# Banded attention: the output projection as plain fp32 matmuls, and four step tables laid out anew

## The chip, the core and the metric

The kernel is one program on one core of a Trainium2 chip. The metric is the device time of one execution in microseconds (us), as the median of the runs shown. Engines are named as in the profile: PE (TensorE matmul), PEld (TensorE weight load, which runs beside PE), DVE (VectorE), ACT (ScalarE), POOL (GpSimd) and SP (SyncE, whose queue issues the DMAs here).

## What is computed

Four layers on an input of 8 sequences of 512 tokens with 256 channels, each added to its input: attention with relative positions, a layer of 16 experts, banded attention, and a second layer of 16 experts. The change is in the third.

```python
q = x @ wq.T; k = x @ wk.T                       # 256 -> 1024 channels, 16 heads of 64
v = (x @ wv.T).reshape(Bx, Tx, H, D).transpose(0, 2, 1, 3)
q = _rmsnorm(q, q_gamma, 1e-06) ...; k = _rmsnorm(k, k_gamma, 1e-06) ...
scores = jnp.einsum('bhqd,bhkd->bhqk', q, k) * scale
scores = scores + slopes[None, :, None, None] * dist[None, None]
mask = (j_minus_i > 0) | (j_minus_i < -WINDOW)   # WINDOW = 128
scores = jnp.where(mask[None, None], -1000000000.0, scores)
attn = jax.nn.softmax(scores, axis=-1)
out = jnp.einsum('bhqk,bhkd->bhqd', attn, v)
out = out.transpose(0, 2, 1, 3).reshape(Bx, Tx, H * D)
return out @ wo.T                                # 1024 -> 256 channels
```

## The kernel before

`window_stage` computes the banded attention. Its tiles carry the prefix b_ in the profile. It works in 32 windows of 128 query tokens: 8 sequences (b), each of 4 windows (t = 0 to 3), where window number w = 4 b + t. A window sees its own 128 keys and the 128 before them; window t = 0 has no keys before it (`lo` = 1), so its scores, softmax, transposes and value products are half as wide.

The engines run the same list of windows, each through a table of its own that is written by hand: `WINDOW_ORDER` (PE), `WINDOW_SCALAR_ORDER` (ACT), `WINDOW_VECTOR_ORDER` (DVE), `WINDOW_POOL_ORDER` (POOL) and `WINDOW_SYNC_ORDER` (SP). An entry is (step, part, offset): the step is done for the window that lies that many windows ahead of or behind the current one. One pass through the tables is called a unit here; PE's unit of window t ends with the second half of `v` for window t + 1. `rounds` writes out the units of sequences 0, 1 and 7, and puts the four units of a sequence into a hardware loop for sequences 2 to 6. So the loop is run five times, and each engine branches back four times; this is called a loop turn.

The steps of PE for one window are `x` (transpose of the normalised input), `q`, `k` and `v` in two halves each (L1483), `q_T` and `k_T` (transposes, L1490), `scores` 0 to 3 (L1548), `probs_T` 0 to 7 (transposes of the softmax, L1556), `values` 0 to 7 (L1567), `out` (the output projection, L1498), `xn_T` and, once for each sequence, `gate` (L1512). All of `x`, `q`, `k`, `v`, `q_T`, `k_T`, `out`, `xn_T` and `gate` write one PSUM bank, `ps_w`. Before each of them `bank_free` waits until the one before was read out. `values` 0 to 3 and 4 to 7 share another bank, `ps_o`, so `values` 4 and the next window's `values` 0 wait until it was read out.

A product that has to be precise is done in three terms: each operand is split into `high` (type fp32r, a CAST on ACT) and `rest` (x minus high, on DVE, `rest_of`, L453), and PE adds high times rest, rest times high and high times high. `q`, `k`, `v` and `out` are done so. The scores, the value products and the transposes are plain fp32. For `out` the chain is: `values` 3 or 7 on PE, ("high", k) on ACT (L1613), ("rest", k) on DVE, which increments `o_taken`; PE waits for `o_taken` before `out` and before `values` 4 and 0. The weights of `out` are split once at the stage's start, as the last of four weights, in `split_weights` on ACT (L1634) and DVE.

Other names that are needed: ("divide", k) on POOL (L1669) multiplies the probabilities of two heads by 1 / sum, and `probs_T` k waits for it; ("inverse", k) on DVE (L1730) is that reciprocal; "pow" and "normed" on POOL (L1658, L1664) make the normalised q and k; "x_pow" on POOL (L1655) and "x_normed" on DVE (L1695) normalise the input of a later window; ("probs_T", k) on DVE (L1734) copies the transposes to SBUF, and `values` k waits for that. `reach_alone` is a wait as an instruction of its own, ahead of the one that needs it.

## Time and profile before

| | us |
|---|---|
| median of 3 runs (lowest to highest) | 3925.07 (3919.52 to 3925.45) |
| the profiled execution, its own time | 3910.7 |
| its span, first to last instruction | 3908.9 |
| `window_stage`, from its first `q` matmul to its last output step | 970 (2128 to 3098) |

The page gives the busy time of each engine over the span, and in 40 slices of it. For this change the stage between 2128 and 3098 us is to be read apart from the rest: its busy times, then the rows of PE in order of time. A row's idle time in brackets is what the engine stood still just before it, with the instruction that let it go on. PE rows overlap: the length of a matmul row is longer than the distance to the next row's start, and it is that distance (called pitch here) that PE is held for. A wait that is shorter than the row ahead of it is not shown as idle time, only as a longer pitch.

### The profile page before, as it was taken

To read this page: it belongs to the slowest core of one execution; us is meant where nothing else is said; L and a number is where in the kernel's file an instruction comes from. 1 tells how busy PE (TensorE), PEld (TensorE's weight loads), DVE (VectorE), ACT (ScalarE), POOL (GpSimd) and SP (SyncE) were. 2 spreads that over 40 slices of the span, in tenths; PEclk is the share of its full clock that TensorE was granted. 3 is DMA by queue.
4 is the path that set the end of the run, shared out by engine and by line. 5 is a ranking of instruction groups with operands and counts; after the bars stand their busy time and mean duration, and the time that the engine had idled before them with its cause. 6 is when DMAs were issued, how large, how long until landed. Compare 5 with 4: busy or idle time off the path is not lost. (4 is left out here: it accounts for less than half of the span.)

```text
span 3908.9 us, 92834 instructions
## 1 busy us (share of the span) xinstructions
PE 3506.8 (90%) x33008; PEld 2695.1 (69%) x33008; DVE 2466.3 (63%) x5459; ACT 1826.1 (47%) x3736; POOL 1036.2 (27%) x1016
## 2 busy tenths in 40 slices
PE   3899999999986786999995999999999795999998
PEld 3566666666655675888884677667667585888887
DVE  5566666666664567676663666666666566666664
ACT  2566666666651323444442555455445432444443
POOL 0122222222220002333331343334333201232332
PEclk9999999999998897999998999999999897999999
DMA  5565666566545323443432000000000122443441
GB/s 189 151 171 167 173 174 173 167 175 175 168 129 180 115 74 126 117 119 109 116 92 82 13 20 18 21 21 18 18 21 19 59 81 100 124 113 103 127 114 32
DMA packets 372911, 407.00 MB, mean 104 GB/s; under 512 B 172689, under 2 KB 314385, under 8 KB 359057
## 3 DMA queue, kind: packets, MB, share of 16 engines
q1 hardware_dynamic: 347922, 368.09, 29.9%
q0 software_dynamic: 24576, 33.57, 4.9%
q8 instruction: 238, 3.90, 0.4%
q14 instruction: 175, 1.43, 0.1%
HBM read 255.49 MB, written 146.08 MB: 103 GB/s over the span
## 5 line engine op out<-in xcount | busy, mean ns | idle before, releaser
L2445 POOL TENSOR_TENSOR a_below<-a_probT,a_upper 128x512 f32<-128x512 f32 x128 | 164.3, 1283 | 724.6 <-ACT a_probT L2369 378.1
L2393 ACT ACTIVATE a_prob<-a_ps_s,a_low 128x512 f32<-128x512 f32 x512 | 319.2, 689 | 48.1 <-DVE a_low L2585 48.1
L1669 POOL TENSOR_TENSOR b_prob<-b_prob,b_rinv 128x512 f32<-128x512 f32 (+1 forms) x256 | 238.3, 935 | 386.5 <-DVE b_rinv L1730 386.3
L2254 PE MATMUL a_ps_p<-a_ident,a_prob 128*128 128x128 f32 x2048 | 309.3, 284 | 13.9 <-ACT a_band L2373 9.0
L2585 DVE TENSOR_REDUCE a_low<-a_ps_s 128x2 f32<-128x1024 f32 x256 | 313.5, 1225 | 8.8
L1607 ACT ACTIVATE b_prob<-b_score,b_low 128x256 f32<-128x256 f32 (+1 forms) x512 | 241.7, 474 | 129.6 <-DVE b_low L1725 113.8
L2254 PEld LDWEIGHTS a_ps_p<-a_ident,a_prob 128*128 128x128 f32 x2048 | 216.4, 141 | 106.1 <-issue 80.6
L2369 ACT COPY a_probT<-a_ps_p 128x512 f32<-128x512 f32 x352 | 193.9, 588 | 154.4 <-PE a_ps_p L2254 154.4
L1725 DVE CUSTOM_DVE_ANT_0 b_score<-b_ps_s,b_bias 128x256 f32<-128x256 f32 (+1 forms) x512 | 178.1, 385 | 74.9 <-PE b_ps_s L1548 71.6
L2584 DVE TENSOR_TENSOR a_ps_s<-a_ps_s,a_win 128x320 f32<-128x320 f32 (+1 forms) x256 | 135.0, 528 | 142.9 <-PE a_ps_s L2287 138.4
L903 POOL DMA_INDIRECT x<-fe_eo,fe_index_scatter x64 | 121.6, 1899 | 361.5 <-DVE fe_eo L1098 346.9
L903 POOL DMA_INDIRECT out<-ge_eo,ge_index_scatter x64 | 120.1, 1876 | 359.9 <-DVE ge_eo L1098 345.3
L490 ACT ACTIVATE fe_gelu<-fe_ps_g 128x512 f32<-128x512 f32 x128 | 76.5, 598 | 287.5 <-PE fe_ps_u L469 287.5
L490 ACT ACTIVATE ge_gelu<-ge_ps_g 128x512 f32<-128x512 f32 x128 | 76.5, 598 | 284.4 <-PE ge_ps_u L469 284.4
L1734 DVE COPY b_probT<-b_ps_p 128x512 f32<-128x512 f32 (+1 forms) x256 | 155.5, 616 | 62.2 <-PE b_ps_p L1556 60.6
L506 DVE TENSOR_TENSOR fe_raw<-fe_gelu,fe_ps_u 128x512 f32<-128x512 f32 x128 | 87.9, 687 | 157.4 <-ACT fe_gelu L490 157.1
L506 DVE TENSOR_TENSOR ge_raw<-ge_gelu,ge_ps_u 128x512 f32<-128x512 f32 x128 | 87.9, 686 | 156.2 <-ACT ge_gelu L490 156.2
L1567 PE MATMUL b_ps_o<-b_probT,b_v 128*64 128x128 f32 x1792 | 150.3, 288 | 4.4 <-DVE b_probT L1734 3.8
L1556 PE MATMUL b_ps_p<-b_ident,b_prob 128*128 128x128 f32 x896 | 148.3, 283 | 5.8 <-POOL b_prob L1669 5.8
L479 PE MATMUL fe_ps_d<-fe_d_rest,fe_h_high 128*128 128x256 f32 x512 | 144.4, 282 | 9.8 <-DVE fe_eo L1098 6.9
L479 PE MATMUL ge_ps_d<-ge_d_rest,ge_h_high 128*128 128x256 f32 x512 | 144.3, 282 | 9.8 <-DVE ge_eo L1098 6.9
L2568 DVE COPY a_probT<-a_ps_p 128x512 f32<-128x512 f32 x160 | 110.4, 691 | 64.7 <-PE a_ps_p L2254 62.1
(426 smaller groups left out, 10402.1 us busy)
## 6 DMA issues: line engine op xcount, KB each, us to landing
a_win<-band SPq DMA_DIRECT2D x128, 384.0 KB, 4.8
prob<-a_prob SPq DMA_DIRECT2D x128, 384.0 KB, 3.6
shift<-a_gbias SPq DMA_DIRECT2D x64, 256.0 KB, 2.1
a_shifted<-shift SPq DMA_DIRECT2D x256, 64.0 KB, 2.0
a_bins<-prob SPq DMA_DIRECT2D x128, 128.0 KB, 3.5
fe_gT<-in_WgT SPq DMA_DIRECT2D x16, 1024.0 KB, 4.9
fe_uT<-in_WuT SPq DMA_DIRECT2D x16, 1024.0 KB, 5.2
fe_dT<-in_WdT SPq DMA_DIRECT2D x16, 1024.0 KB, 4.8
```

The costliest lines, as they stand in the source:

```text
L479: last = nc.tensor.matmul(ps_d[t // 2][:, t % 2, :], h[b][:, slot, t * P:(t + 1) * P], d[a][:, j, :], start=(j == 0 and t % 2 == 0 and (a, ...
L506: nc.vector.tensor_tensor(raw[:, slot % 2, :], gelu[:, slot % 2, :], ps_u[slot % 2][:, :], ALU.mult).then_inc(h_ready, 1)
L903: nc.gpsimd.indirect_dma_start(rows_y, bass.IndirectOffsetOnAxis(index[1][:, q, t:t + 1], 0), eo[:, q, t, :], None, bounds_check=B * T - 1 ...
L1607: nc.scalar.activation(prob[:, h % 8, lo * P:], score[:, h % 8, lo * P:], ACT.Exp, bias=low[:, h % 8:h % 8 + 1], scale=-1.0, accum_out=rsu ...
L1669: nc.gpsimd.tensor_tensor(part, part, by_row, ALU.mult).then_inc(divided, 1)
L1725: nc.vector.tensor_tensor_reduce(out=score[:, h % 8, lo * P:], in0=ps_s[k // 2 % 2][r][:, k % 2, lo * P:], in1=bias[:, h, lo * P:], scale= ...
L1734: nc.vector.tensor_copy(probT[:, k % 2, :, lo:, :], ps_p[k % 2][:, :, lo:, :]).then_inc(copied, 1)
L2254: last = nc.tensor.transpose(bank[:, c * P:(c + 1) * P], prob[:, t % 2, h, 32 + c * P:32 + (c + 1) * P], ident[:, :])
L2369: last = nc.scalar.copy(probT[:, t % 2, h, :], ps_p[i][:, :])
L2393: nc.scalar.activation(prob[:, t % 2, h, 32:32 + T], ps_s[pair][:, r, :], ACT.Exp, bias=low[:, h:h + 1]).then_inc(exped, 1)
L2445: nc.gpsimd.tensor_tensor(below[:, t % 2, :, :], probT[:, t % 2, :, t * P:(t + 1) * P], upper[:, :].unsqueeze(1).to_broadcast([P, HG, P]), ...
L2585: nc.vector.reduce_max(low[:, 2 * pair:2 * pair + 2], both[:, :, :], AX.X, negate=True).then_inc(maxed, 1)
```

## The change

`out` becomes 8 plain fp32 matmuls of 128x256 in place of 24 in three terms. `oT` and `woT` are single fp32 tiles; ("rest", k) on DVE and the split of the weights of `out` on ACT and DVE are gone; ("high", k) on ACT is now a COPY and itself increments `o_taken`. `woT` has a tile of its own and no longer borrows `prob`. The load of `bias` is issued ahead of that of `woT`. The four compute tables and SP's are written anew:

```diff
 WINDOW_ORDER = [
-    ("scores", 0, 0), ("x", 0, 1), ("scores", 1, 0), ("out", 0, -1), ("probs_T", 0, 0), ("q", 0, 1), ("scores", 2, 0), ("q", 1, 1),
...
-    ("values", 7, 0), ("v", 1, 1),
+    ("scores", 0, 0), ("x", 0, 1), ("values", 7, -1), ("scores", 1, 0), ("q", 0, 1), ("scores", 2, 0), ("out", 0, -1), ("probs_T", 0, 0),
...
+    ("values", 6, 0), ("v", 1, 1),
 WINDOW_SCALAR_ORDER = [
-    ("exp", 0, 0), ("exp", 1, 0), ("exp", 2, 0), ("exp", 3, 0), ("exp", 4, 0), ("q", 0, 1), ("q", 1, 1), ("k", 0, 1), ("exp", 5, 0), ("k", 1, 1),
...
+    ("high", 1, -1), ("exp", 0, 0), ("exp", 1, 0), ("gate_exp", 0, -2), ("exp", 2, 0), ("exp", 3, 0), ("exp", 4, 0), ("exp", 5, 0), ("q", 0, 1),
...
 WINDOW_SYNC_ORDER = [
-    ("store", 0, -1), ("store_turned", 0, -2), ("store_normed", 0, -1), ("load", 0, 3),
+    ("store_normed", 0, -2), ("load", 0, 2), ("store", 0, -1), ("store_turned", 0, -2),
 ]
...
-        wo = [s.sb(f"wo_{part}", [P, CH, C], F32R) for part in ("high", "rest")]
+        woT = s.sb("woT", [P, CH, C])
...
-        oT = [s.sb(f"oT_{part}", [P, CH, P], F32R) for part in ("high", "rest")]
+        oT = s.sb("oT", [P, CH, P])
...
             load(0, 1)
-            sp.dma_start(woT.rearrange("p a b -> p (a b)").rearrange("p (k c) -> p k c", k=CH), woT_d).then_inc(wo_in, 16)
             sp.dma_start(bias[:, :, :], bias_d).then_inc(bias_in, 16)
+            sp.dma_start(woT[:, :, :], woT_d).then_inc(wo_in, 16)
...
                 elif kind == "out":
                     pe.wait_ge(o_taken, 2 * w + 2)
                     if isinstance(w, int) and w == 0:
-                        pe.wait_ge(wo_split, 1)
-                    terms = [(c, o_part, w_part) for c in range(CH) for o_part, w_part in ((1, 0), (0, 0), (0, 1))]
-                    for c, o_part, w_part in terms:
-                        last = nc.tensor.matmul(ps_w[:, 0:C], oT[o_part][:, c, :], wo[w_part][:, c, :],
-                                                start=((c, o_part, w_part) == terms[0]), stop=((c, o_part, w_part) == terms[-1]))
+                        pe.wait_ge(wo_in, 16)
+                    for c in range(CH):
+                        last = nc.tensor.matmul(ps_w[:, 0:C], oT[:, c, :], woT[:, c, :], start=(c == 0), stop=(c == CH - 1))
                     last.then_inc(filled["out"], 1)
...
-                        nc.scalar.copy(oT[0][:, 4 * k:4 * k + 4, :].rearrange("p c t -> p (c t)"), ps_o[:, :]).then_inc(o_high, 1)
+                        nc.scalar.copy(oT[:, 4 * k:4 * k + 4, :].rearrange("p c t -> p (c t)"), ps_o[:, :]).then_inc(o_taken, 1)
...
-                act.wait_ge(wo_in, 16)
-                for i in range(0, CH, 2):
-                    flat = woT.rearrange("p a b -> p (a b)")
-                    nc.scalar.copy(wo[0][:, i:i + 2, :].rearrange("p k c -> p (k c)"), flat[:, i * C:(i + 2) * C]).then_inc(wo_high, 1)
...
-                    elif kind == "rest":
-                        dve.wait_ge(o_high, 2 * w + k + 1)
-                        flat = lambda a: a[:, 4 * k:4 * k + 4, :].rearrange("p c t -> p (c t)")
-                        rest_of(nc, flat(oT[1]), ps_o[:, :], flat(oT[0])).then_inc(o_taken, 1)
...
-                for i in range(0, CH, 2):
-                    dve.wait_ge(wo_high, i // 2 + 1)
-                    flat = lambda a: a[:, i:i + 2, :].rearrange("p k c -> p (k c)")
-                    rest = rest_of(nc, flat(wo[1]), woT.rearrange("p a b -> p (a b)")[:, i * C:(i + 2) * C], flat(wo[0]))
-                rest.then_inc(wo_split, 1)
```

In PE's rest of the unit the sequence after `v` 0 is now: `gate`, `values` 2, `q_T` 0, `probs_T` 4, `values` 3, `q_T` 1, `probs_T` 5, `values` 4, `k_T` 0, `probs_T` 6, `values` 5, `k_T` 1, `probs_T` 7, `values` 6, `v` 1. On ACT, `v` 0 now stands ahead of ("exp", 6) and ("exp", 7), and ("high", 0) right behind these.

PE at the start of a full-width window, before: scores 0, x, scores 1, then out (24 matmuls in three terms), probs_T 0 and q 0.

```order
L1548 MATMUL b_ps_s<-b_kT,b_qT 128x256 x4
L1475 MATMUL b_ps_w<-b_ident,b_xn 128x128 x2
L1548 MATMUL b_ps_s<-b_kT,b_qT 128x256 x4
L1498 MATMUL b_ps_w<-b_wo_high,b_oT_rest 128x256
L1498 MATMUL b_ps_w<-b_wo_high,b_oT_high 128x256
...
L1498 MATMUL b_ps_w<-b_wo_rest,b_oT_high 128x256
L1556 MATMUL b_ps_p<-b_ident,b_prob 128x128 x4
L1483 MATMUL b_ps_w<-b_wq_high,b_x_rest 128x512
```

The same place now: L1560 is values 7 of the window before, L1478 is q 0, and L1492 is out.

```order
L1541 MATMUL b_ps_s<-b_kT,b_qT 128x256 x4
L1470 MATMUL b_ps_w<-b_ident,b_xn 128x128 x2
L1560 MATMUL b_ps_o<-b_probT,b_v 64x128 x4
L1541 MATMUL b_ps_s<-b_kT,b_qT 128x256 x4
L1478 MATMUL b_ps_w<-b_wq_high,b_x_rest 128x512
...
L1478 MATMUL b_ps_w<-b_wq_rest,b_x_high 128x512
L1541 MATMUL b_ps_s<-b_kT,b_qT 128x256 x4
L1492 MATMUL b_ps_w<-b_woT,b_oT 128x256 x8
L1549 MATMUL b_ps_p<-b_ident,b_prob 128x128 x4
```

`out` moved behind q 0 and scores 2, and values 7 moved from the end of the unit to the next one's start.

POOL at the end of the loop's body, before: the two parts of normed, with divides 5 and 6 between them and divide 7 behind, then the branch.

```order
L1664 TENSOR_SCALAR b_normed<-b_raw,b_rrms 128x1024
L78 REGISTER_ALU
L1669 TENSOR_TENSOR b_prob<-b_prob,b_rinv 128x512
L78 REGISTER_ALU
L1669 TENSOR_TENSOR b_prob<-b_prob,b_rinv 128x512
L78 REGISTER_ALU
L1664 TENSOR_SCALAR b_normed<-b_raw,b_rrms 128x1024
L78 REGISTER_ALU
L1669 TENSOR_TENSOR b_prob<-b_prob,b_rinv 128x512
L1369 REGISTER_ALU
L1369 COMPARE_AND_BRANCH
```

POOL at the same place now (L1653 is normed, L1658 divide):

```order
L1653 TENSOR_SCALAR b_normed<-b_raw,b_rrms 128x1024
L78 REGISTER_ALU
L1653 TENSOR_SCALAR b_normed<-b_raw,b_rrms 128x1024
L78 REGISTER_ALU
L1658 TENSOR_TENSOR b_prob<-b_prob,b_rinv 128x512
L1364 REGISTER_ALU
L1364 COMPARE_AND_BRANCH
```

Divide 5 is now the last before the branch; divides 6 and 7 of window 3, and x_pow behind them, stand at the start of the body.

DVE at the end of the loop's body and, behind the branch, its first two rows, now (L1700 is q_T 1, L1719 inverse 7, L1723 the copies of probs_T 5 and, after the branch, of 6 and 7, L1684 x_normed):

```order
L1700 TENSOR_TENSOR b_qT<-b_ps_w,b_gains 128x512
L1718 REGISTER_ALU
L1719 RECIPROCAL b_rinv<-b_rsum 128x2
L1721 REGISTER_ALU
L1723 COPY b_probT<-b_ps_p 128x512
L78 REGISTER_ALU
L1684 TENSOR_SCALAR b_xn<-b_x,b_mv,b_rstd 128x256
L1364 REGISTER_ALU
L1364 COMPARE_AND_BRANCH
L1723 COPY b_probT<-b_ps_p 128x512 x2
```

x_normed moved to the end of the unit, behind a wait of its own for x_pow; before, the copy of probs_T 5 was DVE's last row ahead of the branch.

## Rows read from the trace of the kernel before

**Rows 1.** The page: span, and busy time of each engine.

```profile
span 3908.9 us, 92834 instructions
PE 3506.8 (90%) x33008; PEld 2695.1 (69%) x33008; DVE 2466.3 (63%) x5459; ACT 1826.1 (47%) x3736; POOL 1036.2 (27%) x1016
```

**Rows 2.** Busy time by stretch: the stage, three full windows, two t = 0 windows.

```profile
core 0: us, PE busy (x) PEld busy (x) DVE busy (x) ACT busy (x) POOL busy (x), PEclk, DMA share, GB/s
2128.00:3098.00 970.00, 909.14 (x6396) 666.45 (x6397) 611.09 (x2174) 475.07 (x1543) 363.81 (x415) 0.97 0.06 19
2293.00:2378.00 85.00, 84.70 (x625) 62.75 (x624) 59.88 (x205) 45.34 (x144) 36.67 (x39) 1.00 0.06 20
2378.00:2407.00 29.00, 25.88 (x173) 18.54 (x171) 16.11 (x69) 12.70 (x48) 8.84 (x13) 0.94 0.07 20
2485.00:2513.00 28.00, 22.87 (x167) 17.14 (x165) 13.91 (x57) 10.45 (x36) 8.85 (x13) 0.94 0.05 14
```

**Rows 3.** PE in order of time, a full window: scores 0, out, next scores 0.

```profile
start us, us, engine line op out<-in xcount [idle before <-releaser]
2350.03 1.13 PE L1548 MATMUL b_ps_s<-b_kT,b_qT 64*128 64x256 f32 x8
...
2352.56 0.38 PE L1498 MATMUL b_ps_w<-b_wo_high,b_oT_rest 128*128 128x256 f32 x1
...
2355.47 0.60 PE L1556 MATMUL b_ps_p<-b_ident,b_prob 128*128 128x128 f32 x4
...
2378.50 0.71 PE L1548 MATMUL b_ps_s<-b_kT,b_qT 64*128 64x128 f32 x8
```

**Rows 4.** PE in order of time, plain fp32: 512 columns, and eight of 128 columns.

```profile
609.26 1.02 PE L2235 MATMUL a_ps_w<-a_k_low,a_tables 128*128 128x512 f32 x2
610.22 1.08 PE L2296 MATMUL a_ps_o<-a_probT,a_v 128*32 128x128 f32 x32
...
532.38 1.95 PE L2231 MATMUL a_ps_w<-a_wv,a_xT 128*128 128x128 f32 x16
534.26 0.87 PE L2287 MATMUL a_ps_s<-a_k_low,a_q 32*32 32x256 f32 x32
```

**Rows 5.** The removed split of the attention output: its row and its waits.

```profile
L453 DVE TENSOR_TENSOR b_oT_rest<-b_ps_o,b_oT_high x64: 690/692/693, 2174.0 to 3085.4; 128x512 fp32r<-128x512 f32 x64
who waited for it (us, times):
  PE b_ps_w L1498: 1.5, 1
```

**Rows 6.** A full window's end: PE, then DVE, then POOL, each in order of time.

```profile
2340.86 0.66 PE L1567 MATMUL b_ps_o<-b_probT,b_v 128*64 128x128 f32 x8
2347.40 1.09 PE L1567 MATMUL b_ps_o<-b_probT,b_v 128*64 128x128 f32 x16
...
2338.99 0.42 DVE L1725 CUSTOM_DVE_ANT_0 b_score<-b_ps_s,b_bias 128x256 f32<-128x256 f32 x1
...
2339.57 0.70 POOL L1658 TENSOR_TENSOR b_rrms<-b_ms,b_minus_half 128x2 f32<-128x2 f32 x1 [3.30 <-DVE b_ms L1716]
2340.67 1.13 POOL L1664 TENSOR_SCALAR b_normed<-b_raw,b_rrms 128x1024 f32<-128x1024 f32 x1 [0.40 <-POOL b_rrms L1658]
2341.75 2.04 POOL L1669 TENSOR_TENSOR b_prob<-b_prob,b_rinv 128x512 f32<-128x512 f32 x2
```

**Rows 7.** A loop turn: PE, DVE and ACT, each in order of time.

```profile
2493.38 1.25 PE L1567 MATMUL b_ps_o<-b_probT,b_v 128*64 128x128 f32 x16 [1.03 <-DVE b_probT L1734]
...
2498.38 0.71 PE L1548 MATMUL b_ps_s<-b_kT,b_qT 64*128 64x128 f32 x8 [2.14 <-issue]
...
2489.91 0.68 DVE L1734 COPY b_probT<-b_ps_p 128x512 f32<-128x512 f32 x1
2492.64 1.29 DVE L1734 COPY b_probT<-b_ps_p 128x512 f32<-128x512 f32 x2 [2.04 <-PE b_ps_p L1556]
...
2499.49 0.37 ACT L1586 CAST b_x_high<-b_ps_w 128x256 fp32r<-128x256 f32 x1 [2.64 <-PE b_ps_w L1475]
2502.21 0.40 ACT L1607 ACTIVATE b_prob<-b_score,b_low 128x128 f32<-128x128 f32 x1 [2.34 <-issue]
```

**Rows 8.** A t = 0 window, PE in order of time: out, q 0, q 1, gate.

```profile
2380.79 0.38 PE L1498 MATMUL b_ps_w<-b_wo_high,b_oT_rest 128*128 128x256 f32 x1 [0.39 <-DVE b_x_rest L453]
...
2384.38 0.50 PE L1483 MATMUL b_ps_w<-b_wq_high,b_x_rest 128*128 128x512 f32 x1 [0.29 <-DVE b_x L1741]
...
2387.36 0.50 PE L1483 MATMUL b_ps_w<-b_wq_high,b_x_rest 128*128 128x512 f32 x1 [0.67 <-DVE b_raw L1706]
...
2398.24 1.96 PE L1512 MATMUL b_ps_w<-b_gwT,b_ynT 128*128 128x16 f32 x16 [0.31 <-ACT b_v L1596]
```

**Rows 9.** The stage's start: DVE, then PE.

```profile
2125.06 2.49 DVE L453 TENSOR_TENSOR b_wo_rest<-b_prob,b_wo_high 128x512 fp32r<-128x512 f32 x4
2127.47 0.42 DVE L453 TENSOR_TENSOR b_x_rest<-b_ps_w,b_x_high 128x256 fp32r<-128x256 f32 x1
...
2127.99 0.77 PE L1483 MATMUL b_ps_w<-b_wq_high,b_x_rest 128*128 128x512 f32 x1 [11.12 <-DVE b_x_rest L453]
```

**Rows 10.** The stage's end: PE at the last out.

```profile
3086.28 0.35 PE L1498 MATMUL b_ps_w<-b_wo_high,b_oT_rest 128*128 128x256 f32 x1 [1.50 <-DVE b_oT_rest L453]
```

30 lines of the change are left out of this document (13 added, 17 removed).

## Prediction

> **What bounds the kernel now.** The page first: PE is busy 90% of the span, the other engines 63% and less [rows 1]. Next the stage that the change touches, by stretch: from 2128 to 3098 us PE is busy 909 of 970 us, with the granted clock at 0.97 [rows 2]. Then inside the stage. Three full-width windows, 2293 to 2378, have PE busy 84.70 of 85.00 us at clock 1.00: they are closed. The window of t = 0 is not: 25.88 of 29.00 us, and 22.87 of 28.00 where it stands at a loop turn [rows 2]. In order of time a full window lasts 28.47 us, from scores 0 at 2350.03 to the next at 2378.50 [rows 3]. So in 24 of the 32 windows each us that is added to PE is added to the time, and no relief of DVE or ACT gives any back. In the 8 windows of t = 0, about 3 us of idle time could be won.
>
> **1. The output projection on PE, the main term.** Before, 24 matmuls of 128x256 run from 2352.56 to 2355.47, 2.91 us, at full clock [rows 3]. This is 6144 column passes (24 x 256) at 0.47 ns. Now there are 8 plain fp32 matmuls; the trace has none of 128x256. Its two nearest rows, both plain fp32 with 128 weights: one matmul of 512 columns is two records and holds PE 0.96 us, 609.26 to 610.22; eight of 128 columns are 16 records in 1.88 us, 532.38 to 534.26 [rows 4]. Per column of one matmul this is 1.88 and 1.84 ns, so it takes about four times what a three-term matmul's single pass takes (0.47). Eight of 256 columns by these: 8 x 0.48 = 3.84 us, or 16 x 0.235 = 3.76 us. Three passes become four, where the number of instructions falls to a third. The difference is 0.85 to 0.93 us a window; I take 0.88, the middle, since 256 columns lie between the rows. 32 windows: **+28 us** (27 to 30). Nothing covers it: `out` is on PE itself.
>
> One rule of the Trainium skill speaks against this term. Perfetto Trace Analysis, section Engine Utilization, puts the systolic array's output rate at half for FP32_LOW_HIGH. Read as the rate of a whole fp32 matmul, it is a rival below.
>
> **2. The removed split.** ("rest", k) is 64 DVE instructions of 0.69 us, 44 us of DVE, but in the whole stage PE waited for it once, 1.5 us [rows 5]. With PE closed this saves only that one wait, in part 5.
>
> **3. The window's end, where the new order tightens a chain.** Times from the end of v 0 on PE (2340.86, V). In the new order PE has values 2, q_T 0, probs_T 4, values 3, q_T 1, probs_T 5, values 4, k_T 0, probs_T 6, values 5, k_T 1 and probs_T 7 ahead of values 6. They are the same 12 steps, in another order, that PE did between V and 2347.40, so values 6 is wanted at about V + 6.5 [rows 6]. It needs the copy of probs_T 6, which on DVE now stands behind x_normed, and that waits for x_pow on POOL, which stands behind divides 6 and 7. POOL: the mean stood behind biased 6 (second half at 2338.99), and that behind the copy of probs_T 2; this copy now comes later, so the mean is about 0.4 earlier, and pow starts near V - 1.7 in place of 2339.57, normed 0 1.1 later at V - 0.6; then normed twice (1.08 each), divides 5, 6 and 7 (1.02 each), ends V + 4.7; x_pow 0.55, V + 5.2 [rows 6]. The start of x_normed is then V + 5.4; it took 0.78 at most, and the copy 0.6 to 0.7, so the copy is done at V + 6.7 to 6.9. PE stands 0.2 to 0.4 us there, or not at all if one lag is smaller than I put it. I take 0.2 in 24 windows: **+5 us** (0 to 9). In t = 0 windows the divides are half as long, and PE reaches that point later through the gate.
>
> **4. The four loop turns.** The trace shows what a branch back costs: from the start of the last instruction to the start of the next 2.73 us on DVE (2489.91 to 2492.64) and 2.72 on ACT (2499.49 to 2502.21), while PE shows 2.14 idle. Today PE pays 1.03 ahead of values 6 and 7, because DVE's branch stands between the copies of probs_T 5 and 6, and then its own 2.14 [rows 7]. Now DVE branches after x_normed. Even if POOL's branch cost nothing: V + 5.4 + 2.7 + 0.65 = V + 8.8 against V + 6.5, 2.3 idle, 1.3 more than today. POOL's branch is newly on this path, between divides 5 and 6. No row shows its price, since POOL waits 12 us behind it today. Bounds: 0, and the 2.7 of DVE, counted from the start of divide 5 at V + 1.6: divide 6 then starts at V + 4.3 instead of 2.6, and all behind it is 1.7 later: 3.0 more than today. ACT comes on top: its branch stands between x_high and high 1, exp 0. At present exp 0 comes 3.8 us after scores 0 and the out section hides it; in the new order q 0's read-out on DVE stands behind inverse 0, which needs exp 0, and `out` waits for that read-out. High 1 and exp 0 end near 5.3 us after scores 0, inverse 0, biased 2 and the read-out 1.3 later, and `out` could otherwise start at 4.5: up to 2 us, of which half is covered by q 0 running at the lower clock level there (granted clock 0.94 over that window [rows 2]). So 1.3 to 5 a turn. I take 2.5, nearer the end without POOL's branch since the halves overlap: 4 x 2.5 = **+10 us** (5 to 20).
>
> The skill's page on this is Runtime: NRT & Kernel Launch, section Instruction fetch mechanics: a taken branch to a target out of the fetched window stalls on a fetch. It names every engine, POOL too, and gives no duration; it would favour the upper bound.
>
> **5. The rest.** t = 0 windows: `out` waited 0.39 for x_rest and q 1 0.67 for q 0's read-out, which stood late in DVE's table [rows 8]. Values 7 (0.6 us) now covers the first, and the earlier place in DVE's table a part of the second. Against it, gate follows v 0 with nothing between, where values 2 (0.37) left 0.31 idle: 0.7 now. I take -0.4 each, **-3 us** (-8 to +3). Start: the four wo_rest, 2125.06 to 2127.47, stood ahead of x_rest, for which the first q waited [rows 9]: **-2.4 us**. The copy on ACT ends earlier than that and sets nothing. The later load of woT has until the first out, 50 us. End: the last out no longer waits for rest, -0.7 of the 1.5 [rows 10], and is some 1.2 longer beyond its part in term 1, as most of its passes run at the lower clock level there: **+0.5 us** in all. Loads now run two windows ahead in place of three; a window is 28 us, so they stay hidden.
>
> **Sum:** 28 + 5 + 10 - 3 - 2.4 + 0.5 = +38 us. The profiled execution (span 3908.9, own time 3910.7) would be at 3947 and 3949. It lies 14 us under the median of the runs, 3925.07, so I put the difference on the median: **3963 us**.
>
> **Rivals.**
> - *The new order packs the open windows* (the other side). Place: the 8 windows of t = 0, 3.1 us idle each [rows 2], and the 1.03 at each turn. If all of it goes, 25 + 4, no wait of parts 3 and 4 appears, and the start gives 2.4: 28 - 29 - 2.4 + 0.5 = -3, 3922. To be faster by more than 0.2% (8 us) it must also take a part of PE's own 2.14 at turns, or win over 34 us altogether. For: DVE loses 44 us of work and `out` is no longer first after x. Against: the waits inside t = 0 are mostly the read-out of one bank, ps_w, between neighbouring sections, and their cover is as thin as before. Half of it won (3938) is the low side; same 0.09, faster 0.04.
> - *Fp32 at half rate.* Then a 256-column matmul takes two passes, 2 x 0.1175 = 0.235 us, and eight 1.88: 1.03 less than today, -33 us in place of +28. With the other terms: 38 - 61 = -23, 3902. Against: a 512-column matmul would have to hold PE 0.48, and it holds it 0.96 [rows 4]. Chance 0.02. By the skill's rule named in part 1 this would be the result; the trace agrees with it only if it is meant for each of the two records.
> - *Only the projection counts.* Parts 3 and 4 cost nothing: 28 - 3 - 2.4 + 0.5 = +23, 3948. Inside my range.
> - *The chain POOL, DVE, PE is dear.* Each turn 5, each full window 0.36, gate's loss uncovered: 28 + 20 + 9 + 3 - 2 = +58, 3983 and more. Chance above that 0.10.
> - *The split stays in part.* Excluded: the order of PE shows 8 instructions, and no rest is left on DVE.
>
> **How the numbers follow.** Forecast with the two cases inside it, slower by 15 to 59 us: 0.75; dearer 0.10; same 0.09; faster 0.06 (0.04 + 0.02). The range leaves out the dear end and what lies below +16: 3941 to 3984, about 0.8. Within 0.2% is within 8 us of 3925, about what a measurement of this kernel can tell from no change. Faster 0.06, same 0.09, slower 0.85.
>
> **What the profile after would show.** Part 1: from the first record of `out` to the probs_T behind it 3.8 us, in 16 records; if 1.9, the half rate holds. A full window of 29.3 to 29.6 us. Part 3: PE idle 0.2 to 0.4 ahead of values 6, released by the DVE copy; if none, that lag was too long. Part 4: 2.3 to 4 idle ahead of values 6 at a turn, POOL with a gap behind divide 5, and idle time before `out` released by DVE's read-out of q. Part 5: the first q of the stage 2.4 sooner after the weights; gate's idle 0.7. I am wrong above all if the idle time of t = 0 windows shrinks by more than 1 us each, or if a window's end opens by more than 0.5.

## The result and the profile after

| | before | after |
|---|---|---|
| median, us (lowest to highest, 4 runs each) | 3923.2 (3919.5 to 3925.5) | 3971.8 (3969.5 to 3973.9) |
| ratio to before, 95% interval | | 1.0125 (1.0107 to 1.0142) |
| first q to the last record of the last out, us (profiled execution) | 962.5 | 1013.0 |
| a full window, scores 0 to scores 0, us | 28.47 | 29.84 |
| gate to gate, a sequence without a loop turn, us | 114.7 | 120.3 |
| gate to gate, a sequence with one, us (mean of four) | 121.3 | 130.2 |

The changed kernel is slower by 48.6 us. The profiled execution of before is 12 us under the median of its runs. Against that of after it is also 9 us shorter ahead of the stage and 4 behind it, where nothing was changed. So the two are compared stage to stage: +50.5 us, or +48.1 with the wait ahead of the first q, which became 2.4 shorter. "Gate to gate" is the distance from one gate on PE to the next. It spans one sequence, with a loop turn in it or without. One distance of that kind is good to some 2 us: the other one without a turn is 115.7 in before, and 118.6 against 116.5 in plain_old_tables, a kernel further below.

The page after, span and busy times, as in [rows 1], and then the stretches that answer to [rows 2]: the stage, three full windows, a t = 0 window, and a stretch with a loop turn. Ahead of them stands the stage of before once more, cut off at the last record of its last out, as the one of after is:

```profile
span 3971.9 us, 92245 instructions
PE 3550.4 (89%) x32752; PEld 2713.2 (68%) x32752; DVE 2429.8 (61%) x5391; ACT 1822.3 (46%) x3732; POOL 1035.5 (26%) x1016
```

```profile
core 0: us, PE busy (x) PEld busy (x) DVE busy (x) ACT busy (x) POOL busy (x), PEclk, DMA share, GB/s
2128.00:3090.90 962.90, 905.70 (x6380) 663.29 (x6380) 609.50 (x2169) 474.69 (x1542) 363.26 (x414) 0.98 0.06 18
```

```profile
2137.00:3150.00 1013.00, 935.25 (x6124) 673.25 (x6124) 574.16 (x2105) 472.88 (x1542) 362.13 (x414) 0.96 0.06 17
2304.00:2394.00 90.00, 87.62 (x601) 63.28 (x601) 57.73 (x198) 45.30 (x146) 36.55 (x39) 1.00 0.06 19
2394.00:2424.00 30.00, 26.92 (x169) 19.45 (x170) 14.66 (x67) 13.51 (x48) 8.84 (x13) 0.94 0.06 19
2508.00:2553.00 45.00, 37.59 (x218) 27.23 (x215) 18.09 (x74) 15.24 (x54) 12.55 (x18) 0.81 0.04 13
```

The stage became 50.5 us longer, and PE's busy time in it 30 us more (935 against 906). The other 20 are idle time. The full windows are open now: 87.62 of 90 us, where [rows 2] has 84.70 of 85. At the loop turn the granted clock is 0.81.

PE in order of time, a full window of after, against [rows 3] (out, and the three places where PE stands now):

```profile
start us, us, engine line op out<-in xcount [idle before <-releaser]
2334.16 1.13 PE L1541 MATMUL b_ps_s<-b_kT,b_qT 64*128 64x256 f32 x8
...
2339.90 3.72 PE L1492 MATMUL b_ps_w<-b_woT,b_oT 128*128 128x256 f32 x16
2343.45 0.60 PE L1549 MATMUL b_ps_p<-b_ident,b_prob 128*128 128x128 f32 x4
...
2352.28 0.44 PE L1497 MATMUL b_ps_w<-b_ident,b_yn 128*128 128x128 f32 x2 [0.19 <-DVE b_raw L1695]
...
2355.73 0.63 PE L1485 MATMUL b_ps_w<-b_ident,b_normed 128*128 128x128 f32 x4 [0.19 <-POOL b_normed L1653]
...
2361.82 0.66 PE L1560 MATMUL b_ps_o<-b_probT,b_v 128*64 128x128 f32 x8 [0.19 <-DVE b_probT L1723]
2364.00 1.14 PE L1541 MATMUL b_ps_s<-b_kT,b_qT 64*128 64x256 f32 x8
```

The projection holds PE 3.55 us (2339.90 to 2343.45) where it held it 2.91: +0.64. There are 16 records, as forecast. Three waits of 0.19 are new: ahead of xn_T, q_T 0 and values 6. With them 0.64 + 0.57 = 1.21 of the 1.37 us are named. Most of the rest lies ahead of v 0, where PE waits for ACT's copy of xn_T: from probs_T 3 to v 0 it takes 0.74, before 0.62.

A loop turn of after, against [rows 7]: PE, then DVE, ACT and POOL, each in order of time:

```profile
2516.29 1.12 PE L1560 MATMUL b_ps_o<-b_probT,b_v 128*64 128x128 f32 x8 [3.13 <-DVE b_probT L1723]
2517.34 0.80 PE L1478 MATMUL b_ps_w<-b_wv_high,b_x_rest 128*128 128x512 f32 x1
...
2520.20 1.23 PE L1541 MATMUL b_ps_s<-b_kT,b_qT 64*128 64x128 f32 x8
...
2528.02 5.40 PE L1492 MATMUL b_ps_w<-b_woT,b_oT 128*128 128x256 f32 x16 [2.21 <-DVE b_raw L1695]
2533.26 0.38 PE L1549 MATMUL b_ps_p<-b_ident,b_prob 128*128 128x128 f32 x2
...
2512.30 0.41 DVE L1684 TENSOR_SCALAR b_xn<-b_x,b_mv,b_rstd 128x256 f32<-128x256 f32 x1 [1.40 <-POOL b_rstd L1644]
2515.54 1.29 DVE L1723 COPY b_probT<-b_ps_p 128x512 f32<-128x512 f32 x2 [2.83 <-issue]
...
2526.18 0.17 DVE L1719 RECIPROCAL b_rinv<-b_rsum 128x2 f32<-128x2 f32 x1 [2.84 <-ACT b_prob L1600]
...
2527.19 0.69 DVE L1695 COPY b_raw<-b_ps_w 128x512 f32<-128x512 f32 x1
...
2524.79 0.59 ACT L1606 COPY b_oT<-b_ps_o 128x512 f32<-128x512 f32 x1 [2.34 <-issue]
...
2508.18 2.04 POOL L1658 TENSOR_TENSOR b_prob<-b_prob,b_rinv 128x512 f32<-128x512 f32 x2
```

Four things are to be seen. First, PE stands 3.13 us ahead of values 6, for the copies that DVE makes only behind x_normed (2512.30) and its branch (2.83 "issue"). Second, behind v 1 PE goes straight on to scores 0 (2520.20, no idle): its own 2.14 of [rows 7] is gone. Third, out waits 2.21 for q 0's read-out, which stands behind a reciprocal, and that waits for ACT's first exponential, behind ACT's branch (2.34). Fourth, POOL's two divides, one on either side of its branch, fill 2.04 us without a gap: POOL's branch costs nothing. (From the branch to the next record of the same sequencer it is 0.3 us on POOL, 2.7 to 3.1 on DVE and 2.4 to 2.7 on ACT, in every looped kernel of this document.) Behind both of PE's waits the clock is at its lower level: out takes 5.24 us (2528.02 to 2533.26) in place of 3.55. It is so at all four turns of after.

A t = 0 window, PE at out and gate, against [rows 8]; then the first q of the stage and the last out, against [rows 9, 10]. The last line is of before: probs_T 0 of the stage's first window.

```profile
2398.99 3.72 PE L1492 MATMUL b_ps_w<-b_woT,b_oT 128*128 128x256 f32 x16 [0.41 <-DVE b_raw L1695]
...
2414.12 1.96 PE L1505 MATMUL b_ps_w<-b_gwT,b_ynT 128*128 128x16 f32 x16 [0.68 <-ACT b_v L1589]
...
2136.89 0.76 PE L1478 MATMUL b_ps_w<-b_wq_high,b_x_rest 128*128 128x512 f32 x1 [8.71 <-DVE b_x_rest L453]
...
3146.59 3.69 PE L1492 MATMUL b_ps_w<-b_woT,b_oT 128*128 128x256 f32 x16 [0.78 <-ACT b_oT L1606]
```

```profile
2156.62 0.69 PE L1556 MATMUL b_ps_p<-b_ident,b_prob 128*128 128x128 f32 x2 [3.01 <-POOL b_prob L1669]
```

The first q waits 2.4 us less than before (8.71, was 11.12), the last out 0.7 less, gate 0.4 more. The last out runs at full clock now, 3.69 us; before it ended at 3090.9, 4.6 after its start. In the stage's first window, which has no out ahead of it, PE stood 3.01 for POOL's first divide. With q 0 and scores 2 in front of probs_T 0 this wait is gone, and that window is 2.9 us shorter (scores 0 to scores 0, 27.9 and 25.0).

### The profile page after: what moved, and what is told of

It is laid out like the page before. It is cut to its first block and busy times, and to the rows that moved or that the text cites. A ratio compares the mean times of both kernels' runs of the same rounds, so it can differ in the third digit from the quotient of the medians.

```text
span 3971.9 us, 92245 instructions
## 1 busy us (share of the span) xinstructions
PE 3550.4 (89%) x32752; PEld 2713.2 (68%) x32752; DVE 2429.8 (61%) x5391; ACT 1822.3 (46%) x3732; POOL 1035.5 (26%) x1016
## 5 line engine op out<-in xcount | busy, mean ns | idle before, releaser
L1658 POOL TENSOR_TENSOR b_prob<-b_prob,b_rinv 128x512 f32<-128x512 f32 (+1 forms) x256 | 237.3, 935 | 501.1 <-DVE b_rinv L1719 500.4
L1714 DVE CUSTOM_DVE_ANT_0 b_score<-b_ps_s,b_bias 128x256 f32<-128x256 f32 (+1 forms) x512 | 178.2, 383 | 112.4 <-PE b_ps_s L1541 107.0
L1560 PE MATMUL b_ps_o<-b_probT,b_v 128*64 128x128 f32 x1792 | 157.8, 292 | 19.3 <-DVE b_probT L1723 19.1
L1723 DVE COPY b_probT<-b_ps_p 128x512 f32<-128x512 f32 (+1 forms) x256 | 154.9, 615 | 19.2 <-issue 11.4
L2276 PEld LDWEIGHTS a_ps_o<-a_probT,a_v 128*32 128x32 f32 x4096 | 104.2, 109 | 57.5 <-ACT a_probT L2349 45.0
```

The costliest lines, as they stand in the source:

```text
L1658: nc.gpsimd.tensor_tensor(part, part, by_row, ALU.mult).then_inc(divided, 1)
L1714: nc.vector.tensor_tensor_reduce(out=score[:, h % 8, lo * P:], in0=ps_s[k // 2 % 2][r][:, k % 2, lo * P:], in1=bias[:, h, lo * P:], scale= ...
```

## The experiments

All times below are medians. Each ratio is to runs of the kernel before beside it, whose median was 3920.8 for the first four kernels, 3923.5 for the next four, 3925.1 for the next two and 3921.8 for the last.

| kernel | us | ratio (95% interval) | gate to gate without / with a turn |
|---|---|---|---|
| plain_old_tables | 3918.6 | 0.9989 (0.9978 to 0.9999) | 116.5 / 119.1 |
| new_tables_24 | 3951.3 | 1.0074 (1.0057 to 1.0091) | 118.0 / 126.8 |
| old_unrolled | 3897.2 | 0.9937 (0.9917 to 0.9957) | 114.4 / none |
| new_unrolled | 3928.6 | 1.0018 (1.0008 to 1.0029) | 120.0 / none |
| plain_old_padded | 3941.0 | 1.0045 (1.0028 to 1.0062) | 118.1 / 125.0 |
| plain_old_unrolled | 3906.8 | 0.9960 (0.9945 to 0.9974) | 116.5 / none |
| new_xn_early | 3940.1 | 1.0051 (1.0033 to 1.0068) | 119.7 / 124.4 |
| new_q_before_inverse | 3953.0 | 1.0080 (1.0065 to 1.0094) | 120.2 / 125.8 |
| new_xn_q | 3932.9 | 1.0014 (1.0001 to 1.0027) | 119.5 / 121.3 |
| new_xn_q_gate | 3947.2 | 1.0059 (1.0038 to 1.0080) | 122.8 / 124.1 |
| old_two_terms | 3894.9 | 0.9932 (0.9914 to 0.9950) | 112.4 / 117.6 |

(For before these are 114.7 / 121.3, for after 120.3 / 130.2. "Without" is the first interval, or for an unrolled kernel the mean of the first six; "with" is the mean of four.)

### The arithmetic alone, and the tables alone

The theory was that of the prediction, with the price as after shows it: the projection costs PE 0.63 us a window (A), and the tables cost the rest. The rival: the change of arithmetic does it all (B), or the tables do. One kernel has the changed arithmetic with the tables of before:

```diff
 WINDOW_ORDER ... WINDOW_SYNC_ORDER: those of before
-    ("rest", 1, -1), ... ("rest", 0, 0),
```

> The new output projection (8 plain fp32 matmuls, no split) under the step tables of before, with only the two rest entries taken out. Theory A (the tables cost more than the matmuls): out takes 3.56 us in the trace of after against 2.93 in that of before, so 32 x 0.63 = +20, less 2.4 at the start: 3941. Full windows 29.0 us. Rival B (the plain fp32 matmuls carry all the loss, and waits come with them under any table): as after, 3972, full windows 29.8.

It took 3918.6 us, the time of before: both theories missed. Out had its 3.56 us, and a full window 28.9. So the longer projection is there, though a full window grew by only 0.4, and something at the turns gives it back: a sequence without a turn is 1.8 us longer than before, one with a turn 2.1 shorter. PE at that turn:

```profile
2511.51 1.26 PE L1560 MATMUL b_ps_o<-b_probT,b_v 128*64 128x128 f32 x16 [1.05 <-DVE b_probT L1723]
...
2514.28 0.72 PE L1541 MATMUL b_ps_s<-b_kT,b_qT 64*128 64x128 f32 x8
```

Against [rows 7] the wait of 1.0 ahead of values 6 is the same, but PE's own 2.14 ahead of scores 0 is gone, here too. This was not foreseen, and the next part is about it.

The mirror of it has the new tables and 24 one-pass matmuls. It leaves out the rest of the attention output (the high part is taken twice):

```diff
-terms = [(c, o_part, w_part) for c in range(CH) for o_part, w_part in ((1, 0), (0, 0), (0, 1))]
+terms = [(c, 0, w_part) for c in range(CH) for w_part in (0, 1, 0)]
```

> The new tables with 24 one-pass fp32r matmuls for out; the split of the weights is kept, that of the attention output is left out, so the term of its rest is missing and high times high is added twice: the result is not the reference's. It has the new tables' waits and the old projection's time on PE. Theory A: after less 32 x 0.63 = 20, plus 2.4 for the weights' split: 3954, with the same waits at the end of a full window (values 6, q_T 0, xn_T, 0.8 us together). Rival B (the waits come from the longer out): 3925, windows of 28.4. Rival C (the shorter out only lengthens the waits): 3972.

It came out as theory A expected. The tables alone cost 30.5 us, and the arithmetic in them 3971.8 - 3951.3 = 20.5, where 32 x 0.64 less the 2.4 of the start would be 18. PE at its turn, then the branches back of PE's sequencer (PEldq; five of them, shortest, median and longest in ns, the shortest being the last one, which isn't taken):

```profile
2506.76 1.12 PE L1569 MATMUL b_ps_o<-b_probT,b_v 128*64 128x128 f32 x8 [3.22 <-DVE b_probT L1736]
...
2510.96 1.23 PE L1550 MATMUL b_ps_s<-b_kT,b_qT 64*128 64x128 f32 x8 [0.22 <-issue]
```

```profile
L1369 PEldq COMPARE_BRANCH  x5: 83/3522/3587, 2507.0 to 3012.4; - x5
```

The 3.2 us wait is the tables'. Behind it PE's own idle is 0.22 and not 2.14. The branch lasts 3.59 us here too, from 2507.0 on, so it begins behind the wait. But PE has values 6 and v 1 to work off meanwhile, and at the lower clock level these take it from 2506.76 to 2510.96. Before, the branch began at 2494.2 and v 1 ended at 2496.2. So in the new tables the removal of that idle is worth next to nothing, and in the old ones 12 us by the unrolled pairs, or up to 17 by the gate distances (both below).

### With the loop written out

```diff
-            for b in range(2):
-                for t in range(NT):
-                    unit(b, t)
-            with engine.Fori(2, B - 1) as b:
-                for t in range(NT):
-                    unit(b, t)
-            for t in range(NT):
-                unit(B - 1, t)
+            for b in range(B):
+                for t in range(NT):
+                    unit(b, t)
```

> The kernel before with the hardware loop over sequences written out, so that no engine branches back. Theory: a sequence with a turn takes 121.3 us from gate to gate and one without 115.2, so 4 x 6 = 24 less: 3899. Rival: the time is that of fetching instructions and comes back in the straight program: 3923.

> The changed kernel with the loop written out. Gate to gate a sequence with a turn takes 130.2 us and one without 120.2: 4 x 10 = 40 less, 3932, so that the change costs 33 without turns and 16 through them. Rival: turns cost both kernels the same 24: 3948.

Both as expected. The four turns cost 3920.8 - 3897.2 = 23.6 us before the change, 5.9 each, and 3971.8 - 3928.6 = 43.2 after it, 10.8 each. So 19.6 us of the change are turns, and 31.4 (3928.6 - 3897.2) are there without any. (The sum is 51.0, since runs beside each other give 3920.8 for before.) old_unrolled beats both kernels.

### Why PE's own idle went

Theory C: at a branch back PE has to load its loop body again if it doesn't fit, and the change made the body smaller. The out sections of a body (4 units) have 96 matmul records with three terms and 64 with plain fp32, and each has a weight load beside it. Rival D: the order around the turn or the kind of matmul. The test puts the size back, by five tiny matmuls for each projection (104 records in a body):

```diff
+                    for i in range(5):
+                        nc.tensor.matmul(ps_w[0:32, 0:4], oT[:, i, 0:32], woT[:, i, 0:4], start=True, stop=True)
                     for c in range(CH):
```

> The kernel plain_old_tables with five tiny fp32 matmuls (32 weight columns, 4 columns moved) ahead of the eight of each output projection, so that TensorE's loop body has about as many instructions again as before the change. The question: TensorE's own idle of 2.1 us at each turn of the loop, which the profile of before shows and that of plain_old_tables (3918.6 us) does not. Theory C, the body's size decides whether the branch back stalls TensorE: the idle of about 2.1 us with no releaser stands ahead of scores 0 at each of the four turns again, the sequences with a turn are 4 to 6 us longer than the ones without, the packets on the instruction queue go back towards 238 from 201, and the time is about 3918 + 8 for the added matmuls (0.25 us a window) + 18 = 3944 us. Rival D, the idle went for another reason (the order around the turn): only the added matmuls cost, 3926 us, and the sequences with a turn are longer than the others by no more than the 2.2 us they are in plain_old_tables.

3941.0 us, near the 3944 of theory C, but part of that agreement is luck. The five tiny matmuls cost 0.41 us in a full window (out section 3.97 against 3.56), not 0.25, so 13 us in all. That leaves 9 of the 22.4 for the turns, where 18 were expected; rival D comes to 3932 by this price. What decides is the trace. PE at its turn:

```profile
2516.53 0.72 PE L1543 MATMUL b_ps_s<-b_kT,b_qT 64*128 64x128 f32 x8 [2.19 <-issue]
...
2519.22 5.17 PE L1494 MATMUL b_ps_w<-b_woT,b_oT 128*128 128x256 f32 x16
2524.23 0.38 PE L1551 MATMUL b_ps_p<-b_ident,b_prob 128*128 128x128 f32 x2
```

The idle is back (2.19), and behind it the projection runs at the lower clock level, 5.01 us instead of 3.56. So a stall of 2.2 us costs more than its length at this turn. A sequence with a turn is 6.9 us longer than one without, against 2.7 in plain_old_tables: 17 us in four turns by these distances, 9 by the medians.

The branch itself shows the two cases directly. PE's sequencer in before, plain_old_tables, plain_old_padded, and in old_two_terms (below):

```profile
L1369 PEldq COMPARE_BRANCH  x5: 76/3593/3782, 2494.2 to 2978.4; - x5
...
L1364 PEldq COMPARE_BRANCH  x5: 76/208/208, 2512.3 to 2989.9; - x5
...
L1364 PEldq COMPARE_BRANCH  x5: 83/3465/3821, 2512.3 to 3010.4; - x5
...
L1369 PEldq COMPARE_BRANCH  x5: 83/215/215, 2496.6 to 2965.9; - x5
```

A taken branch lasts 3.3 to 3.8 us with the large body and 0.21 with the small one. What PE still has queued up covers a part of it, and 1.7 to 2.2 us of idle time are left in before and in plain_old_padded.

The instruction queue of the page's part 3 shows the same (queue, then packets, MB and share): before and plain_old_padded have the first line, plain_old_tables the second.

```profile
q8 instruction: 238, 3.90, 0.4%
```

```profile
q8 instruction: 201, 3.29, 0.3%
```

The smaller body saves 37 packets, 0.61 MB, and a packet is 16.4 KB (3.90 MB / 238), so about 9 a turn. new_tables_24, with the large body, has 238. After, and every other looped kernel with 64 records, has 201.

The Trainium skill has this in Runtime: NRT & Kernel Launch, section Instruction fetch mechanics: instructions are refilled in 16 KiB blocks of 256, PE's memory has 128 KiB (2048 instructions), and a taken branch stalls if its target isn't in the current window of two pages. The packet size agrees with it, and so does the stall of the large body. By its figures a whole PE memory is 8 blocks, an estimate close to the 9 a turn here. The two pages do not agree with PE: the body of after has about 1530 matmul and load records (an estimate: an eighth of the stage's 12248, as a body is 4 of its 32 windows), three times two pages of 256, and its branch takes 0.21 us. The limit seen lies between that body and the one of before, some 1600 records by the same count and some 180 records of the sequencer more in either. Why it lies there, below the 2048, no run shows. For the others the two pages are 512 instructions. POOL's body, 172 records with the sequencer's, is within them and its branch costs nothing, so the page did not favour the upper bound of the prediction's part 4. ACT's, 353, is within them too, and pays at every turn. The durations are this trace's; the page has none.

The same question from the other side, with the arithmetic of before but one term less. It leaves out the product with the weights' rest:

```diff
-terms = [(c, o_part, w_part) for c in range(CH) for o_part, w_part in ((1, 0), (0, 0), (0, 1))]
+terms = [(c, o_part, w_part) for c in range(CH) for o_part, w_part in ((1, 0), (0, 0))]
```

> The kernel before with the third term of the output projection left out (the product of the high part with the rest of the weights): 16 one-pass matmuls instead of 24, the orders, the split and everything else untouched. It leaves that part of the computation out. Its TensorE loop body has 32 matmuls less than before, as many matmul and load records as the body with plain fp32. Theory C (the body's size decides whether the branch back stalls TensorE): besides the 8 x 0.12 = 0.98 us of each projection (32 of them = 31 us) the idle of 2.14 us with no releaser at the four turns goes, with the half-clock projection behind it: 18 us more, 3923 - 49 = 3874 us; the instruction queue falls from 238 packets to about 201, and sequences with a turn are within 2.5 us of those without. Rival D (plain fp32 matmuls, not the size, made the idle go): the idle stays, only the matmuls count: 3892 us, 238 packets, turn sequences 6 us longer than the others.

Half of theory C came true. The instruction queue is at 201 packets, the branch takes 0.21 us, and PE's idle ahead of scores 0 is gone, with one-pass matmuls: it isn't their kind. But the time is 3894.9 us, the rival's, and turns still cost 5 us:

```profile
2498.51 0.71 PE L1548 MATMUL b_ps_s<-b_kT,b_qT 64*128 64x128 f32 x8
...
2504.53 0.43 PE L1556 MATMUL b_ps_p<-b_ident,b_prob 128*128 128x128 f32 x2 [1.57 <-POOL b_prob L1669]
2505.93 0.50 PE L1483 MATMUL b_ps_w<-b_wq_high,b_x_rest 128*128 128x512 f32 x1 [0.97 <-DVE b_x L1741]
```

Here out lasts only 1.9 us, and scores 0 comes 2.1 sooner. probs_T 0 then waits 1.57 for POOL's first divide, and q 0 waits 0.97 where it waited 0.29 [rows 8]. By these rows PE needs some 3.5 us of work (1.9 + 1.57) in front of probs_T 0 in the old order to cover the branches of the others. The plain projection of 3.55 gives it, and probs_T 0 doesn't wait in plain_old_tables; one of 1.9 us does not. So a stall that goes is worth what the next engine leaves of it: nothing here (3921.8 less 32 x 0.94 for the shorter out is 3892), 12 us in plain_old_tables.

With no turns, the arithmetic shows its own price:

> The kernel plain_old_tables with the loop over sequences written out. Without turns what is left against old_unrolled (3897 us) is the price of the arithmetic alone. Theory C (TensorE's stall at the turn had already gone with its smaller body): the turns of plain_old_tables cost only the 1.0 us wait ahead of values 6 and little more, 2.2 us each, so writing them out gives 9 us: 3909 us, and the change of arithmetic costs 0.5 us a full window, 12 to 14 us in all, when turns are out of the way. Rival D (turns cost as much as before the change): writing the loop out gives 23.6 us as it did for the kernel before: 3895 us.

As theory C expected: 3906.8 us. Against old_unrolled that is 9.6 us, and a sequence is 2.1 us longer (116.5 against 114.4), less than 4 x 0.64 = 2.6. So even in the old order a part of the longer projection falls into waits that PE had anyway. Against plain_old_tables the unrolling gave 11.8 us, 2.9 a turn, where the kernel before had 5.9. The half that is missing, 11.8 us in four turns, is what the smaller body was worth there.

### Which waits the new tables brought

Theory: at the turn two chains hold PE, x_pow on POOL to x_normed to DVE's branch to the copies for values 6, and ACT's branch to the first exponential to the reciprocal to q 0's read-out to out. Each is cut on its own.

```diff
 VECTOR:  ("x_mean", 0, 2), ("biased", 5, 0),
+         ("x_var", 0, 2),
 ...      ("y_normed", 0, -1), ("k", 1, 1),
+         ("x_normed", 0, 2),
 ...
-         ("x_var", 0, 2),    (behind q_T 0)
-         ("x_normed", 0, 2), (the last)
 POOL:
-         ("x_pow", 0, 1), ahead of divide 0
+         ("x_pow", 0, 2), behind divide 3
```

> The changed kernel with three steps moved to where the old orders had them: VectorE's x_var behind biased 5 and x_normed behind k 1's read-out, GpSimd's x_pow behind divide 3 of the window before. Theory A (as predicted in part 3 and 4: the probs_T copies ahead of values 6 wait behind x_normed, and that behind x_pow): the 0.19 us wait ahead of values 6 and its slower pitch go, 0.3 us in each of 24 full windows = 7; at the turn the 3.1 us wait ahead of values 6 shrinks to the 1.0 of before, 1.5 to 2 us net in each of four since TensorE's own fetch shows again = 6: 3959 us. Rival: the wait is handed to the next place (probs_T or values 7), or x_normed on VectorE delays k 1 and the score steps: 3970 us.

3940.1 us: the theory's direction, at nearly three times its size (-31.7 us where 12 were expected). PE at its turn:

```profile
2500.76 0.66 PE L1560 MATMUL b_ps_o<-b_probT,b_v 128*64 128x128 f32 x8 [0.71 <-DVE b_probT L1723]
2501.34 0.50 PE L1478 MATMUL b_ps_w<-b_wv_high,b_x_rest 128*128 128x512 f32 x1
...
2510.16 5.40 PE L1492 MATMUL b_ps_w<-b_woT,b_oT 128*128 128x256 f32 x16 [2.51 <-DVE b_raw L1695]
2515.40 0.38 PE L1549 MATMUL b_ps_p<-b_ident,b_prob 128*128 128x128 f32 x2
```

The wait ahead of values 6 fell from 3.13 to 0.71. With it went the lower clock behind it (the first v record takes 0.50 here, 0.80 in after), and PE's own idle did not come back, since the body is small. The expectation had counted the wait against a stall that wasn't there, and left the clock out. The second wait is untouched: 2.51, and 5.24 us of projection. The lower clock doesn't follow such a wait every time, though. At the fourth turn of this kernel out waited 2.65 and then ran at full clock (a row of 3.71, as in a full window, not of 5.40):

```profile
2884.04 3.71 PE L1492 MATMUL b_ps_w<-b_woT,b_oT 128*128 128x256 f32 x16 [2.65 <-DVE b_raw L1695]
```

Nor does it need one. In new_unrolled, without turns and with no wait over 0.68 us between the gates, a t = 0 window has such a stretch with PE busy throughout (columns as for the stretches of after; the 0.50 is the granted clock):

```profile
2417.50:2420.90 3.40, 3.36 (x18) 2.30 (x18) 1.98 (x7) 0.59 (x1) 1.42 (x3) 0.50 0.00 0
```

The other chain, cut at DVE by moving the read-out ahead of the reciprocal:

```diff
-    ("biased", 1, 0), ("inverse", 0, 0), ("biased", 2, 0), ("q", 0, 1),
+    ("biased", 1, 0), ("biased", 2, 0), ("q", 0, 1), ("inverse", 0, 0),
```

> The changed kernel with q 0's read-out on VectorE put ahead of the first reciprocal (inverse 0), a swap of two neighbours and biased 2. Theory A: at the turn the wait of 2.2 us ahead of the output projection is a chain: ScalarE's idle of 2.34 us at its branch, then its first exponentials, then VectorE's reciprocal that waits for them, then q 0's read-out behind it, then out. With the read-out ahead of the reciprocal the chain is cut at VectorE, out waits 0.5 us or less, four turns give 1.7 each and some low clock, and nothing changes in full windows: 3963 us. Rival: out is held by ScalarE's copy of the attention output (which comes behind the same branch) for as long: the wait stays near 2 us and is now put down to b_oT, 3971 us.

3953.0 us, 18.8 less than after. The theory holds, but it was 10 us short in size. PE at its turn, DVE's copy ahead of it:

```profile
2522.90 0.69 DVE L1695 COPY b_raw<-b_ps_w 128x512 f32<-128x512 f32 x1 [0.93 <-PE b_ps_w L1478]
...
2523.73 3.72 PE L1492 MATMUL b_ps_w<-b_woT,b_oT 128*128 128x256 f32 x16 [0.41 <-DVE b_raw L1695]
```

The copy now waits for PE and no longer for ACT, out waits 0.41 instead of 2.21, and it runs at full clock, 3.55 us to the next row: 1.8 + 1.7 a turn. Both together:

> The changed kernel with both moves at once: x_var, x_normed and x_pow early, and q 0's read-out on VectorE ahead of the first reciprocal. In new_xn_early (3940 us) the turn still has a 2.51 us wait ahead of the output projection and behind it a projection at the lower clock (5.24 us start to start instead of 3.56). Theory A (the two waits of the turn are separate costs, each with the low clock that follows it): the second goes as it did in new_q_before_inverse, four turns give 2.1 + 1.7 each = 15: 3925 us. Rival (the waits share one limit, the branches of the other engines, and what one frees the next takes): 3937 us.

3932.9 us, the ratio 1.0014: 8 us more than expected, though the turns are as expected: such sequences are 1.8 us longer than the ones without. The granted clock over the first turn is 1.00, where after had 0.81:

```profile
2500.00:2545.00 45.00, 39.91 (x284) 28.79 (x281) 25.55 (x95) 20.34 (x69) 16.47 (x21) 1.00 0.06 19
```

So some 40 us of the change's 48.6 were the two chains (3932.9 is 7.8 above the runs of before beside it), most of that at turns. What is left is in the sequences without a turn, 119.5 us against 114.7. The last kernel tried to get that back too:

```diff
-("gate", 0, -1), ("values", 2, 0), ("q_T", 0, 1), ("probs_T", 4, 0),
+("values", 2, 0), ("gate", 0, -1), ("probs_T", 4, 0), ("q_T", 0, 1),
 and on DVE probs_T 4's copy ahead of q_T 0's read-out
```

> As new_xn_q, and in the middle of the window values 2 goes back between v 0 and the gate, and probs_T 4 back ahead of q_T 0 (on VectorE too). Theory A (small waits of full windows are real terms of the sum): q_T 0's wait on GpSimd's normed (0.21 in each full window) goes and its pitch with it, 0.25 x 24 = 6, and the gate's wait falls from 0.68 to 0.31 in seven windows = 3: 9 us less than new_xn_q, 3916 us. Rival: TensorE's order is tight enough there that the wait moves to the next section (q_T 1 or k_T 0) and the gain is under 3 us: 3923 us.

It was 14 us slower than new_xn_q. Both theory and rival missed: the wait moved on, but grew. PE in a full window:

```profile
2320.85 0.66 PE L1485 MATMUL b_ps_w<-b_ident,b_normed 128*128 128x128 f32 x4 [0.88 <-DVE b_qT L1700]
```

q_T 0's read-out now comes behind a copy on DVE, and q_T 1, which stands only one step behind q_T 0 in this table, waits 0.88 for it. That is up to 21 us in 24 windows. Whether another order of the middle would close the window was not tried.

## Why the prediction was right, and where it was not

The time lay inside the range, and the sign and the main mechanism were right: PE was closed, so what was added to PE was added to the time. The sum of +38 was 11 under the 48.6. By its own parts:

**1. The projection: +28 forecast, +20 measured.** The number of records and passes was right. The mis-sized term is the price of one record: 3.55 / 16 = 0.222 us, not 0.235 or 0.24. The step that failed was how the two rows of other widths [rows 4] were scaled. The whole distance of each holds one change to the next group, and the change was multiplied along with the rest. One record of 512 columns lasts 0.59 (the line below is of before), and the row of two 1.02, so the second starts 0.43 after the first; only from there to the next group it is 0.52. Half of 0.43 is 0.216 for 256 columns, and 16 of these with one change of 0.1 are 3.55. So the rows of before held the right price.

```profile
L2235 PE MATMUL a_ps_w<-a_k_low,a_tables x192: 592/595/1061, 94.2 to 1097.4; 128*128 128x512 f32 x192
```

A one-pass record of 256 columns takes 2.91 / 24 = 0.121 us, so one of plain fp32 costs a little less than two of them (0.242). Plain fp32 is 22% dearer than three terms here, not 30%. The rival of the half rate is out: it asked for 1.9 us.

**2. The split: right.** Its one wait, of 1.5 us ahead of the last out, fell to 0.78.

**3. The window's end: +5 forecast, about +17 found.** The wait ahead of values 6 is 0.19, as taken (0.2). The failing step was to follow one chain only. The new order also has xn_T and q_T 0 standing 0.19 each, for k 1's read-out and for normed, so a full window lost 1.37 - 0.64 = 0.73 beside the projection. In all 24 this would be 17.5; those of sequence 0 lost 0.2 to 0.5, some others up to 1.0. The end of the range, 9, did not hold it.

**4. Turns: +10 forecast, 13 to 20 found.** By the gate distances it is 3.3 a turn (130.2 - 121.3 = 8.9, less the 5.6 of a sequence without one), by the unrolled pair 4.9. Both waits came where they were put: ahead of values 6 released by the DVE copy (2.3 forecast, 3.13 measured), and out by q 0's read-out (up to 2 forecast, 2.21 measured). POOL's branch cost nothing, so the lower bound was the right one there. Two things were missed. PE's own 2.14 disappeared, since the body became smaller; in the new order that is worth little, as new_tables_24 shows (0.22). And in after each wait had a stretch at the lower clock level behind it: the projection 1.7 us longer, and v 1 and the scores slower as well. The prediction let the lower clock cover a part of a wait, and never put it down as a price.

**5. The rest: -5 forecast, about -4 found.** The start was right to 0.1 (-2.4), and so was the wait of the last out (-0.7). That this out would be 1.2 longer beyond its part in term 1 was wrong: it ran at full clock and is 0.9 shorter in all, so 1.6 shorter beyond that part. Gate's wait of 0.68 came as said (0.7). But the t = 0 windows, put down with -0.4 each, lost, all but the first. A sequence without a turn is 5.6 longer, three full windows of it 4.1, which leaves 1.5, or 0.9 beyond the projection. Scores 0 to scores 0 the three of them without a turn lost 0.7 to 1.8, 0.5 beyond it on average, so some 4 us in seven windows. The first window of the stage won 2.9, or 3.5 beyond the projection, by a wait that the prediction had not looked at. In a t = 0 window with an out of its own ahead, out waits 0.41 as it did before, now for q 0's read-out in place of x_rest: a step put ahead of it to cover one wait brought the next. The old values 2 ahead of gate is gone, and nothing took its place.

**Sum as measured:** 20 + 17 + 13 - 4 = 46, against 48.1 in the profiled executions and 48.6 in the medians (with the 20 of the unrolled pair for turns, 53). Part 1 was 8 too dear and parts 3 and 4 together 15 too cheap, and in part 5 a term of the right size came from other places than forecast. So it is partly luck that the sum was only 11 off. Not settled is the up to 9 us by which stage lengths and medians disagree: new_unrolled and old_unrolled are 38 us apart in the stage of the profiled executions and 31.4 in the medians, plain_old_padded and plain_old_tables 31 and 22.4. Each kernel has one profiled execution only.

The rival that only the projection counts (3948) is refuted by new_tables_24; the new order that packs open windows is refuted by the same kernel, which is slower by 30 us with no plain fp32 in its projection. It held in one place only, the stage's first window.

## What to carry to other kernels

Price an fp32 matmul in place of a three-term one by the distance from one record to the next, at the very width or scaled by columns, and count the change to the next group once. Let the range go below twice the one-pass record. When a table is rewritten, go through every place where neighbours share a bank or a queue, not only the one you suspect: three waits of 0.19 in a window cost as much as the arithmetic. At a loop turn let the range of each wait reach to the slower clock that can follow it. Look at how long the branch record of the sequencer lasts: here it told the large body from the small one in every trace, and the idle time behind it did not (0.22 in new_tables_24).
